# Seven 512-column GpSimd operations of a graph network kernel made into halves of 256 columns

## The chip, the cores and the metric

The kernel runs on one core of one Trainium2 chip. The metric is the device time of one launch in microseconds. The core has five engines that run side by side and meet only through semaphores: TensorE (matrix products into PSUM), VectorE, ScalarE (called ACT in the profile), GpSimd (POOL) and SyncE (SP), whose queue issues the DMAs here.

## What is computed

128 graphs, each with 128 nodes and 256 features, go through four graph layers. Each layer is preceded by a layer normalisation with relu and followed by a residual add. Cut to what matters here:

```python
h = relu(layernorm(x))                         # x: [128, 128, 256], adj: [128, 128, 128]
x = x + L0(h, adj)    # hypergraph conv 256->512, relu, layer norm over 512, conv 512->256, + its input
h = relu(layernorm(x))
x = x + L1(h, adj)    # attention: softmax of masked leaky-relu logits, times Wh, elu
h = relu(layernorm(x))
# L2: diffusion with K = 3
e = leaky_relu(sj[:, None, :] + si[:, :, None] + ab)
alpha = A * exp(e)                             # the edge mask
transition = alpha / (sum(alpha, -1) + 1e-12)
H = sum_k Xk @ Wk[k] + bk[k],  Xk = transition @ Xk
x = x + relu(H)
h = relu(layernorm(x))
x = x + L3(h, adj)    # softmax weight for each node, times a value product
```

All is float32. A large product is made of three: an operand is split into a rounded high part and the low part that is left (value minus high part), and high x high, low x high and high x low are added up in PSUM.

## The kernel before, in words

Four graphs make a group (G = 4), so a tile of a group is 128 partitions by 4 x 128 columns for an adjacency and 4 x 256 for features. There are 32 groups. The work on a group is spread over four rounds like a pipeline: in round i the engines do "next" for group i+1 (layer 0's normalisation, adjacency), "front" for group i (layers 0 and 1), "mid" for group i-1 (layer 2), "late" and "tail" for groups i-2 and i-3 (layer 3 and the store). The middle rounds are a hardware loop (`Fori`), those at both ends are written out. Each engine has a `body(r)` in which the order of its steps is written by hand, and each step waits on counting semaphores (`S[...]`). An engine works strictly in that order.

GpSimd's order within a round is: the low parts of `hT` for chunks 0 to 2 (L832; chunk 3 is VectorE's, L1086), each after ScalarE's `hT_hi` of that chunk; the reciprocal root of layer 2 (`rsqrt`: a small add L782 and a power L784); the sums of the squares `sq` (L788 twice, L841 once), each L788 after a ScalarE square of two chunks; the output add into `x4` (L846, four of 256 columns); the roots of layers 0, 3 and 4 (4 is the norm inside layer L0, `hmean`), with two small steps for `nmr` between; the edge mask `alT = zb * adj_m` (L861); four adds into `xb` (L866); the bias adds on `p0` (L794), the root of layer 1, the adds into `x3n` (L879) and `res0` (L885).

VectorE has in the same round: the layer 2 normalisation (`centred(2, ...)`: moments L973 and L977, and `h` L991, four of 256 columns), its low parts, the sums `hs` of the `hT` chunks (L1091 of 1024 columns, L1093 of 512), `wcol`, the moments of the next input, `sij`, `sjc`, the layer 4 normalisation with the same lines on `x3n`, the leaky relu of `zb` (L1070), the variance of the inner norm (L1098 to L1105), `z` (L1112) which needs the root of `hmean`, the adjacency steps of the next group (L1000 to L1010, with a 4-column copy L1004 and the products `binc_T` L1010), `p1` (L1080), `x1` (L1120) and so on.

Who needs what the changed lines make: TensorE's products on `hT_lo` (`front_w2`, L315) wait for `hT_lo`, its sums over partitions (`front_sums`, L296 on `ones` and `hsq`) for `sq_done`, and its products with the mask (`mid_ap`) for `al_ready`. TensorE's transposes (L384) wait for `h`, and its `front_c2` for `z`.

Of the kernel before, what the change touches and what calls it, by code (L numbers as in the profile page):

```python
# [7 lines left out]
ALU = mybir.AluOpType  # L8
# [56 lines left out]
def wait(eng, sem, value):  # L65

    if value is not None:
        eng.wait_ge(sem, value)


def gnn_stack(nc, x, adjT, w1T, w2T, cols, rows, l1_w, l2_wv, l2_wk, wvT, wqkT, out):
    N, C, D = x.shape
# [3 lines left out]
    G = 4  # L76
# [16 lines left out]
    with ExitStack() as ctx:  # L93
        def sb(name, *shape):
            return ctx.enter_context(nc.sbuf_tensor(name, [P, *shape], F32))

        def split(name, *shape):


            return [ctx.enter_context(nc.sbuf_tensor(f"{name}_{part}", [P, *shape], F32R)) for part in ("hi", "lo")]  # L100

        def sem(name):
            return ctx.enter_context(nc.semaphore(name))
# [23 lines left out]
        adj_m = sb("adj_m", G, C)  # L127
# [17 lines left out]
        hT = sb("hT", HC, G * C)  # L145
        hTs = split("hT", HC, G * C)
        hsq = sb("hsq", HC + 2, G * C)
        sq, hs = hsq[:, 0:HC, :], hsq[:, HC:HC + 2, :]
# [19 lines left out]
        zb = sb("zb", G, C)  # L168
        alT = sb("alT", G, C)
# [51 lines left out]
        S = {n: sem(n) for n in names}  # L221
# [555 lines left out]
        @block.gpsimd  # L777
        def _(pool):
            def rsqrt(layer, src, ready, value, mid, done):

                pool.wait_ge(ready, value)
                pool.tensor_scalar(var_e[:, layer, :], src, EPS_LN, None, ALU.add).then_inc(mid, G)  # L782
                pool.wait_ge(mid, value)
                pool.tensor_tensor(rs[:, layer, :], var_e[:, layer, :], neg_half[:], ALU.pow).then_inc(done, G)  # L784

            def add_squares(r, k):
                pool.wait_ge(S["sq_step"], r.front(2 * k + 2))
                pool.tensor_tensor(sq[:, 2 * k, :], sq[:, 2 * k, :], sq[:, 2 * k + 1, :],  # L788
                                   ALU.add).then_inc(S["sq_half"], G // 2)

            def add_bias(r, b):
                for g in (2 * b, 2 * b + 1):
                    pool.wait_ge(S["p0_copied"], r.mid(g + 1))
                    pool.tensor_tensor(p0[:, g, :], p0[:, g, :], bk[:], ALU.add).then_inc(S["p0b_ready"], 1)  # L794

            def constants():
                pool.memset(ones[:], 1.0).then_inc(S["consts_made"], 1)
                pool.memset(ident[:], 0.0).then_inc(S["pool_zero"], 1)
                pool.wait_ge(S["pool_zero"], 1)
                pool.affine_select(ident[:], ident[:], [[-1, P]], ALU.not_equal, 1.0, base=0,  # L800
                                   channel_multiplier=1).then_inc(S["consts_made"], 1)
                pool.memset(mean_w[:], 1.0 / DH).then_inc(S["consts_made"], 1)
                pool.memset(neg_half[:], -0.5).then_inc(S["consts_made"], 1)
                pool.memset(p2[:, :, D:D + 1], 1.0).then_inc(S["consts_made"], 1)
                pool.wait_ge(S["consts_made"], 5)
                pool.wait_ge(S["b2_loaded"], 16)

                pool.tensor_scalar(b2m1[:], b2m1[:], -1.0, None, ALU.add).then_inc(S["rows_used"], 1)
                pool.wait_ge(S["rows_used"], 1)

            def setup():

                def low(hi, lo, raw, n):
                    pool.wait_ge(S["weights_hi"], n)
                    pool.tensor_tensor(lo, raw, hi, ALU.subtract).then_inc(S["weights_lo"], 1)

                low(w1s[0][:], w1s[1][:], raw_w1, 1)
                low(wl1s[0][:, :, 0:D], wl1s[1][:, :, 0:D], raw_l1, 2)
                for k, at in enumerate((K2, K1, K0)):
                    low(wl2s[0][:, :, at:at + D], wl2s[1][:, :, at:at + D], raw_wk[:, k], 3 + k)  # L820
                low(wl3s[0][:], wl3s[1][:], raw_l3, 7)
                pool.wait_ge(S["weights_lo"], 6)
                pool.memset(c0[:, 4:5], 0.0).then_inc(S["set_pool"], 1)
                pool.wait_ge(S["set_pool"], 1)
                pool.wait_ge(S["set_dve"], 1)

            def body(r):
                if r.has_front:

                    for hc in range(HC - 1):  # L830
                        pool.wait_ge(S["hT_hi"], r.front(hc + 1))
                        pool.tensor_tensor(hTs[1][:, hc, :], hT[:, hc, :], hTs[0][:, hc, :],  # L832
                                           ALU.subtract).then_inc(S["hT_lo"], 1 if hc else 2)
                if r.has_mid:
                    rsqrt(2, mv[:, 2, :, 1], S["ag2"], r.mid(G), S["var2"], S["rs2_ready"])
                if r.has_front:

                    add_squares(r, 0)
                    add_squares(r, 1)
                    pool.wait_ge(S["sq_half"], r.front(G))  # L840
                    pool.tensor_tensor(sq[:, 0, :], sq[:, 0, :], sq[:, 2, :], ALU.add).then_inc(S["sq_done"], G)  # L841
                if r.has_tail:

                    pool.wait_ge(S["vw_ready"], r.tail(G))
                    for g in range(G):
                        pool.tensor_tensor(x4[:, g, :], x4[:, g, :], x3[:, g, :], ALU.add).then_inc(S["x4_ready"], 1)  # L846
                if r.has_next:
                    rsqrt(0, mv[:, 0, :, 1], S["ag0"], r.next(G), S["var0"], S["rs0_ready"])
                    pool.tensor_scalar(nmr[:, 0, :], mv[:, 0, :, 0], -1.0, None, ALU.mult).then_inc(S["nm0"], G)
                    pool.wait_ge(S["rs0_ready"], r.next(G))  # L850
                    pool.wait_ge(S["nm0"], r.next(G))
                    pool.tensor_tensor(nmr[:, 1, :], nmr[:, 0, :], rs[:, 0, :],
                                       ALU.mult).then_inc(S["nmr_ready"], G)
                if r.has_late:
                    rsqrt(3, mv[:, 3, :, 1], S["ag3"], r.late(G), S["var3"], S["rs3_ready"])
                if r.has_front:
                    rsqrt(4, hmean[:, 2, :], S["hvar_ready"], r.front(G), S["vare_h"], S["rsh_ready"])
                if r.has_mid:
                    pool.wait_ge(S["adj_m_loaded"], r.loads(r.i - 1))
                    pool.wait_ge(S["eb_ready"], r.mid(G))  # L860
                    pool.tensor_tensor(alT[:], zb[:], adj_m[:], ALU.mult).then_inc(S["al_ready"], G)  # L861
                if r.has_next:

                    pool.wait_ge(S["x_loaded"], r.loads(r.i + 1))
                    for g in range(G):
                        pool.tensor_tensor(xb[:, g, :], x_in[:, g, :], b2m1[:], ALU.add).then_inc(S["xb_ready"], 1)  # L866
                if r.has_mid:
                    add_bias(r, 0)
                if r.has_front:
                    rsqrt(1, mv[:, 1, :, 1], S["ag1"], r.front(G), S["var1"], S["rs1_ready"])  # L870
                if r.has_mid:
                    add_bias(r, 1)
                if r.has_mid:

                    wait(pool, S["h3_ready"], r.late(G))
                    wait(pool, S["x3_moved"], r.late(G))
                    pool.wait_ge(S["relu_ready"], r.mid(G))
                    for g in range(G):
                        pool.tensor_tensor(x3n[:, g, :], p0[:, g, :], x2[:, g, :], ALU.add).then_inc(S["x3_ready"], 1)  # L879
                if r.has_next:  # L880

                    for g in range(G):
                        pool.wait_ge(S["h0_ready"], r.next(g + 1))
                        pool.wait_ge(S["xb_ready"], r.next(g + 1))
                        pool.tensor_tensor(res0[:, g, :], xb[:, g, :], h0[:, g, :], ALU.add).then_inc(S["res0_ready"], 1)  # L885

            constants()
            rounds(pool, body, setup)


# [445 lines left out]
```

## Time and profile before

| what | us |
|---|---|
| median of 3 runs | 1645.03 (1644.6 to 1646.78) |
| the profiled execution | 1647.62 |
| its span | 1645.7 |
| one round of the loop in it | 48.67 |
| TensorE / VectorE / GpSimd / ScalarE busy | 1504.6 / 1408.9 / 1054.1 / 982.4 |
| granted TensorE clock, mean share of full speed | 0.979 |

The profile is of one execution of its own. Starts are in us from the start of its span, durations of single instructions are its too; times of runs are taken without it. DVE is VectorE, ACT ScalarE, POOL GpSimd, PE TensorE's products and PEld its weight loads. A number such as L832 is a line of the kernel. Where an instruction waits inside an engine (for a memory port, say), the profile shows it as a longer duration and not as idle time; a wait for a semaphore shows as idle time with the instruction that ended it.

### The profile page before, as it was taken

To read this page: it belongs to the slowest core of one execution; us is meant where nothing else is said; L and a number is where in the kernel's file an instruction comes from. 1 tells how busy PE (TensorE), PEld (TensorE's weight loads), DVE (VectorE), ACT (ScalarE), POOL (GpSimd) and SP (SyncE) were. 2 spreads that over 40 slices of the span, in tenths; PEclk is the share of its full clock that TensorE was granted. 3 is DMA by queue.
4 is the path that set the end of the run, shared out by engine and by line. 5 is a ranking of instruction groups with operands and counts; after the bars stand their busy time and mean duration, and the time that the engine had idled before them with its cause. 6 is when DMAs were issued, how large, how long until landed. Compare 5 with 4: busy or idle time off the path is not lost.

```text
span 1645.7 us, 34999 instructions
## 1 busy us (share of the span) xinstructions
PE 1504.6 (91%) x9936; PEld 1327.4 (81%) x9936; DVE 1408.9 (86%) x3980; ACT 982.4 (60%) x2153; POOL 1054.1 (64%) x1266
## 2 busy tenths in 40 slices
PE   3889999999999999999999999999999999999974
PEld 3778888888888888888888888888888888888864
DVE  6688889888889988888988888998888898888853
ACT  3345675655666665567565566656566756556643
POOL 4565676666676666667666667666766766666633
PEclk9799999999999999999999999999999999999987
DMA  4000111100111110111110011111011101001000
GB/s 144 20 15 19 46 46 33 45 31 26 45 45 45 32 45 19 38 45 45 32 45 28 30 45 45 45 32 45 15 43 45 45 32 45 26 31 45 26 26 33
DMA packets 75362, 63.21 MB, mean 38 GB/s; under 512 B 2880, under 2 KB 70848, under 8 KB 75200
## 3 DMA queue, kind: packets, MB, share of 16 engines
q1 hardware_dynamic: 75328, 62.80, 11.7%
q8 instruction: 16, 0.26, 0.1%
q14 instruction: 18, 0.15, 0.0%
HBM read 37.62 MB, written 16.78 MB: 33 GB/s over the span
## 4 chain that ended last, share of the span: by engine, by line
DVE 41%; issue 20%; PE 15%; POOL 13%; ACT 9%; DVEq 1%; POOLq 0%; ACTq 0%
DVE stats L973 6%; PE ps L311 6%; POOL rs L784 6%; POOL x L846 5%; DVE h L991 5%; PE ps L315 3%; PE ps L296 3%; DVE z L1112 3%; ACT wh L624 2%; DVE x L1120 2%; ACT pT L744 2%; DVE mv L977 2%; DVE p L1080 2%; PE ps L384 2%; DVE hsq L1091 2%
## 5 line engine op out<-in xcount | busy, mean ns | idle before, releaser
L624 ACT ACTIVATE p<-ps,rs 128x256 f32<-128x256 f32 x384 | 154.4, 478 | 225.1 <-PE ps L315 196.7
L794 POOL TENSOR_TENSOR p<-p,bk 128x256 f32<-128x256 f32 x128 | 92.8, 746 | 240.2 <-ACT p L624 240.2
L832 POOL TENSOR_TENSOR hT_lo<-hT,hT_hi 128x512 fp32r<-128x512 f32 x96 | 125.6, 1313 | 132.1 <-ACT hT_hi L641 121.1
L784 POOL TENSOR_TENSOR rs<-var_e,neg_half 128x4 f32<-128x4 f32 x160 | 187.0, 1169 | 23.7
L384 PE MATMUL ps<-ident,h 128*128 128x128 f32 x768 | 137.9, 289 | 51.4 <-DVE h L991 47.7
L311 PE MATMUL ps<-wl_hi,h2T_hi 128*128 128x256 f32 (+1 forms) x768 | 174.3, 309 | 1.4 <-DVE h2T_lo L895 1.4
L384 PEld LDWEIGHTS ps<-ident,h 128*128 128x128 f32 x768 | 83.4, 142 | 98.8 <-DVE h L991 96.6
L991 DVE TENSOR_SCALAR h<-x,mv 128x256 f32<-128x256 f32 x256 | 155.6, 627 | 2.2
L315 PE MATMUL ps<-wl_hi,h2T_lo 128*128 128x256 f32 (+1 forms) x768 | 155.5, 284 | 0.0
L311 PE MATMUL ps<-wl_lo,h2T_hi 128*128 128x256 f32 (+1 forms) x768 | 155.2, 284 | 0.0
L879 POOL TENSOR_TENSOR x3n<-p,x 128x256 f32<-128x256 f32 x128 | 100.8, 818 | 71.3 <-ACT p L737 71.3
L296 PE MATMUL ps<-p,alT 128*128 128x256 f32 (+1 forms) x512 | 127.6, 391 | 20.0 <-POOL alT L861 15.3
L296 PEld LDWEIGHTS ps<-p,alT 128*128 128x128 f32 x512 | 92.2, 189 | 52.0 <-POOL alT L861 24.6
L788 POOL TENSOR_TENSOR hsq<-hsq 128x512 f32<-128x512 f32 x64 | 124.3, 1960 | 11.3 <-ACT hsq L634 11.3
L624 ACT ACTIVATE vqk<-ps,rs 128x384 f32<-128x384 f32 x128 | 73.2, 572 | 91.9 <-PE ps L315 91.8
L311 PEld LDWEIGHTS ps<-wl_hi,h2T_hi 128*128 128x128 f32 x768 | 121.0, 191 | 3.7 <-ACT h2T_hi L677 1.5
L315 PEld LDWEIGHTS ps<-wl_hi,h2T_lo 128*128 128x128 f32 x768 | 119.3, 191 | 0.0
L311 PEld LDWEIGHTS ps<-wl_lo,h2T_hi 128*128 128x128 f32 x768 | 119.3, 191 | 0.0
L973 DVE BATCH_NORM_STATS2 stats<-x 128x6 f32<-128x256 f32 x256 | 108.7, 425 | 5.5
L641 ACT ACTIVATE hT<-ps,cols_sb 128x512 f32<-128x512 f32 x128 | 87.2, 682 | 31.3 <-PE ps L315 30.3
L846 POOL TENSOR_TENSOR x<-x 128x256 f32<-128x256 f32 x128 | 91.3, 746 | 20.5 <-ACT x L624 20.5
L311 PE MATMUL ps<-w_hi,hT_hi 128*128 128x256 f32 x512 | 89.9, 298 | 8.3 <-DVE c L960 8.3
(168 smaller groups left out, 4537.7 us busy)
## 6 DMA issues: line engine op xcount, KB each, us to landing
x_in<-in_x SPq DMA_DIRECT2D x32, 512.0 KB, 4.4
out_x<-x SPq DMA_DIRECT2D x32, 512.0 KB, 2.8
adj_f<-in_adjT SPq DMA_DIRECT2D x32, 256.0 KB, 3.5
adj_m<-in_adjT SPq DMA_DIRECT2D x32, 256.0 KB, 2.8
adj_l<-adj_m SPq DMA_DIRECT2D x32, 256.0 KB, 2.3
hsq<-in_rows SPq DMA_DIRECT2D x1, 1152.5 KB, 9.7
vqk<-in_l_wk SPq DMA_DIRECT2D x3, 256.0 KB, 8.4
x<-in_w1T SPq DMA_DIRECT2D x1, 512.0 KB, 6.3
```

The costliest lines, as they stand in the source:

```text
L296: last = pe.matmul(dst, lhsT(c), rhs(c), start=(c == 0), stop=(c == chunks - 1))
L311: pe.matmul(dst, lhsT(a, c), rhs(b, c), start=(a == b == c == 0), stop=False)
L315: last = pe.matmul(dst, lhsT(1 - late, c), rhs(late, c), start=False, stop=(c == chunks - 1))
L384: last = pe.transpose(ps[:, banks[g // 2], ((g % 2) * KC + c) * P:((g % 2) * KC + c + 1) * P], h[:, g, c * P:(c + 1) * P], ident[:])
L624: return act.activation(dst, src, ACT.Copy, scale=scale)
L784: pool.tensor_tensor(rs[:, layer, :], var_e[:, layer, :], neg_half[:], ALU.pow).then_inc(done, G)
L788: pool.tensor_tensor(sq[:, 2 * k, :], sq[:, 2 * k, :], sq[:, 2 * k + 1, :], ALU.add).then_inc(S["sq_half"], G // 2)
L832: pool.tensor_tensor(hTs[1][:, hc, :], hT[:, hc, :], hTs[0][:, hc, :], ALU.subtract).then_inc(S["hT_lo"], 1 if hc else 2)
L846: pool.tensor_tensor(x4[:, g, :], x4[:, g, :], x3[:, g, :], ALU.add).then_inc(S["x4_ready"], 1)
L879: pool.tensor_tensor(x3n[:, g, :], p0[:, g, :], x2[:, g, :], ALU.add).then_inc(S["x3_ready"], 1)
L973: dve.bn_stats(stats[:, layer, g, :], src[:, g, :]).then_inc(st, 1)
L991: dve.tensor_scalar(dst[:, g, :], src[:, g, :], mv[:, layer, g, 0:1], 0.0, ALU.subtract, ALU.max).then_inc(done, 1)
```

## The change

Every place where GpSimd worked on 512 columns in one operation within the rounds now does it in two operations of 256 columns: the three low parts of `hT`, the two sums of pairs of squares, the sum of those two, and the edge mask. These are 7 operations a round, and 14 after it. Only the last of the two signals, with the same amount as before. No wait is added or taken away, and nothing else is moved.

```diff
             def add_squares(r, k):
                 pool.wait_ge(S["sq_step"], r.front(2 * k + 2))
-                pool.tensor_tensor(sq[:, 2 * k, :], sq[:, 2 * k, :], sq[:, 2 * k + 1, :],
-                                   ALU.add).then_inc(S["sq_half"], G // 2)
+                for half in (slice(0, 2 * C), slice(2 * C, G * C)):
+                    last = pool.tensor_tensor(sq[:, 2 * k, half], sq[:, 2 * k, half], sq[:, 2 * k + 1, half], ALU.add)
+                last.then_inc(S["sq_half"], G // 2)
...
                     for hc in range(HC - 1):
                         pool.wait_ge(S["hT_hi"], r.front(hc + 1))
-                        pool.tensor_tensor(hTs[1][:, hc, :], hT[:, hc, :], hTs[0][:, hc, :],
-                                           ALU.subtract).then_inc(S["hT_lo"], 1 if hc else 2)
+                        for half in (slice(0, 2 * C), slice(2 * C, G * C)):
+                            last = pool.tensor_tensor(hTs[1][:, hc, half], hT[:, hc, half], hTs[0][:, hc, half],
+                                                      ALU.subtract)
+                        last.then_inc(S["hT_lo"], 1 if hc else 2)
...
                     pool.wait_ge(S["sq_half"], r.front(G))
-                    pool.tensor_tensor(sq[:, 0, :], sq[:, 0, :], sq[:, 2, :], ALU.add).then_inc(S["sq_done"], G)
+                    for half in (slice(0, 2 * C), slice(2 * C, G * C)):
+                        last = pool.tensor_tensor(sq[:, 0, half], sq[:, 0, half], sq[:, 2, half], ALU.add)
+                    last.then_inc(S["sq_done"], G)
...
                     pool.wait_ge(S["eb_ready"], r.mid(G))
-                    pool.tensor_tensor(alT[:], zb[:], adj_m[:], ALU.mult).then_inc(S["al_ready"], G)
+                    for g in range(0, G, 2):
+                        last = pool.tensor_tensor(alT[:, g:g + 2, :], zb[:, g:g + 2, :], adj_m[:, g:g + 2, :], ALU.mult)
+                    last.then_inc(S["al_ready"], G)
```

## Rows read from the trace of the kernel before

**Rows 1.** The page: span, busy time (share of the span) xinstructions, chain that ended last.
```profile
span 1645.7 us, 34999 instructions
...
PE 1504.6 (91%) x9936; PEld 1327.4 (81%) x9936; DVE 1408.9 (86%) x3980; ACT 982.4 (60%) x2153; POOL 1054.1 (64%) x1266
...
DVE 41%; issue 20%; PE 15%; POOL 13%; ACT 9%; DVEq 1%; POOLq 0%; ACTq 0%
DVE stats L973 6%; PE ps L311 6%; POOL rs L784 6%; POOL x L846 5%; DVE h L991 5%; PE ps L315 3%; PE ps L296 3%; DVE z L1112 3%; ACT wh L624 2%; DVE x L1120 2%; ACT pT L744 2%; DVE mv L977 2%; DVE p L1080 2%; PE ps L384 2%; DVE hsq L1091 2%
```

**Rows 2.** Busy us of two rounds; GpSimd's `xb` (busy, mean ns); `h` (ns min/median/max).
```profile
845.70:894.37 48.67, 46.16 (x312) 40.73 (x311) 43.52 (x123) 30.44 (x68) 32.65 (x39) 1.00 0.12 38
894.37:943.04 48.67, 46.18 (x312) 40.76 (x311) 43.53 (x123) 30.45 (x68) 32.63 (x39) 1.00 0.11 38
...
L866 POOL TENSOR_TENSOR xb<-x_in,b2m 128x256 f32<-128x256 f32 x128 | 89.5, 732 | 0.0
...
L991 DVE TENSOR_SCALAR h<-x,mv x256: 320/354/1372, 64.1 to 1587.0; 128x256 f32<-128x256 f32 x128
```

**Rows 3.** Waits: who waited for whom: us in total, times, longest us.
```profile
PEld ps L384 <- DVE h L991: 96.6, 163, 4.6
...
DVE z L1112 <- POOL rs L784: 41.5, 30, 1.6
...
PEld ps L296 <- POOL alT L861: 24.6, 29, 1.0
```

**Rows 4.** Timeline of one round, GpSimd: start us, us, what, [idle before].
```profile
857.76 1.29 POOL L832 TENSOR_TENSOR hT_lo<-hT,hT_hi 128x512 fp32r<-128x512 f32 x1
...
859.04 1.28 POOL L832 TENSOR_TENSOR hT_lo<-hT,hT_hi 128x512 fp32r<-128x512 f32 x1
...
876.71 1.29 POOL L861 TENSOR_TENSOR alT<-zb,adj_m 128x512 f32<-128x512 f32 x1
877.95 2.80 POOL L866 TENSOR_TENSOR xb<-x_in,b2m 128x256 f32<-128x256 f32 x4
```

**Rows 5.** Timeline of the same round, VectorE, the four `h` of layer 2.
```profile
858.02 1.18 DVE L991 TENSOR_SCALAR h<-x,mv 128x256 f32<-128x256 f32 x1
...
859.54 0.93 DVE L991 TENSOR_SCALAR h<-x,mv 128x256 f32<-128x256 f32 x1
...
860.86 0.35 DVE L991 TENSOR_SCALAR h<-x,mv 128x256 f32<-128x256 f32 x1
```

**Rows 6.** Timeline of the same round: first square sum on GpSimd, first `z` on VectorE.
```profile
863.49 2.25 POOL L788 TENSOR_TENSOR hsq<-hsq 128x512 f32<-128x512 f32 x1 [0.33 <-ACT hsq L634]
...
876.86 0.88 DVE L1112 SCALAR_TENSOR_TENSOR z<-ps,rs,bw 128x256 f32<-128x256 f32 x2 [1.39 <-POOL rs L784]
```

**Rows 7.** Timeline of the same round, VectorE, the sums of `hT`.
```profile
863.39 1.20 DVE L1091 TENSOR_TENSOR hsq<-hT 128x1024 f32<-128x1024 f32 x1
...
864.69 1.60 DVE L1093 TENSOR_TENSOR hsq<-hsq 128x512 f32<-128x512 f32 x1
```

**Rows 8.** Timeline, later in that round: two 256-column adds on GpSimd, two `h`.
```profile
887.61 0.73 POOL L794 TENSOR_TENSOR p<-p,bk 128x256 f32<-128x256 f32 x1 [6.85 <-ACT p L624]
...
888.30 0.77 POOL L794 TENSOR_TENSOR p<-p,bk 128x256 f32<-128x256 f32 x1
...
887.67 1.55 DVE L991 TENSOR_SCALAR h<-x,mv 128x256 f32<-128x256 f32 x2
```

**Rows 9.** Timeline of the same round: VectorE's copy and first `binc_T`, TensorE's second pair on `z`.
```profile
879.34 0.74 DVE L1004 COPY binc_T<-adj_f 128x4 f32<-128x4 f32 x1
...
882.27 0.48 PE L296 MATMUL ps<-z,gt 128*128 128x256 f32 x1 [0.31 <-DVE z L1112]
```

**Rows 10.** Timeline of the same round: root of layer 2, root of layer 0, `zb`.
```profile
861.45 1.71 POOL L784 TENSOR_TENSOR rs<-var_e,neg_half 128x4 f32<-128x4 f32 x1
...
872.08 1.04 POOL L784 TENSOR_TENSOR rs<-var_e,neg_half 128x4 f32<-128x4 f32 x1
...
872.50 0.68 DVE L1070 SCALAR_TENSOR_TENSOR zb<-zb 128x512 f32<-128x512 f32 x1
```

## The prediction

> **What bounds the kernel now.** I read the page first, then the waits, then one round of the loop instruction by instruction. The loop over graph groups repeats every 48.67 us, with the same busy times on every engine in neighbouring rounds [rows 2], so one round stands for all of them. The page has TensorE busy for 91% of the span and VectorE for 86% [rows 1], but a share is not a bound. The chain that ended last spends 41% of the span on VectorE, 20% on issue, 15% on TensorE and 13% on GpSimd, and the largest GpSimd entries in it are `rs` (L784, 6%) and `x` (L846, 5%) [rows 1]. The waits say where: VectorE's `z` waits for GpSimd's `rs` 30 times, 41.5 us in all, once a round, so 1.4 us a round; TensorE's transposes wait for VectorE's `h` (96.6 us, by the weight loads); TensorE waits for `alT`, 24.6 us [rows 3].
>
> In time order a round has three parts that matter here. First, 856.4 to 861.2: GpSimd makes the three low parts of `hT` while VectorE makes the four `h` of layer 2. Second, 863.5 to 876.7: GpSimd adds the squares and then works with hardly a gap through the output adds and four reciprocal roots; `z` starts at 876.86, when the last root is done [rows 4, 6]. In this part GpSimd is the bound, VectorE has 1.4 us to spare. Third, 876.7 to 881.4: GpSimd multiplies the mask, then adds `xb`, while VectorE prepares the next adjacency and ends in the second pair of `z`.
>
> **What a busy port costs, from the rows.** The first `h` starts at 858.02 and takes 1.18 us, while the shortest `h` of the run takes 0.32 us. It ends at 859.20, and the GpSimd operation under which it began ran from 857.76 to 859.05. The second `h` starts at 859.54, ends at 860.47, and the GpSimd operation beside it ended at 860.32 [rows 4, 5]. Both end 0.15 us after the GpSimd operation. The other way round, the first square sum starts at 863.49 under VectorE's 1024-column sum (863.39 to 864.59) and takes 2.25 us in place of the 1.29 of `alT` [rows 4]; VectorE's next sum (864.69) then waits for that one and takes 1.60 us; it ends at 866.29, 0.55 after it [rows 6, 7]. So each of the two engines waits for the end of the other's operation, and comes in between two GpSimd operations that stand back to back: this holds also where they have 256 columns (two `p` adds at 887.61 and 888.30, each holding an `h` that ends about 0.15 after it) [rows 8].
>
> **The change, part by part.** Seven operations of 512 columns a round become fourteen of 256.
>
> Price of one split. Durations: 1.29 us for the 512 columns of `alT` [rows 4], 0.73 for the 256 of `xb` [rows 2], so 0.73 x 2 - 1.29 = 0.17. By start to start: `alT` at 876.71, next operation at 877.95, 1.24; four `xb` from 877.95 to 880.75, 2.80 less the overlap of about 0.05, so 0.69 each [rows 4]; 2 x 0.69 - 1.24 = 0.13. I take 0.13, since in a series what counts is when the next can start. The Trainium skill ("Perfetto Trace Analysis", GPSIMD Engine Instruction) says to time GpSimd by the spacing of starts and not by reported durations. By durations the three splits below would cost 0.51 rather than 0.39, which would put the time 3 to 4 us higher.
>
> 1. Low parts (3 splits, L832). Halves start at about 856.36, 857.05, 857.76, 858.45, 859.14 and 859.83, and the last ends near 860.6 instead of 860.32; TensorE needs them for products that read `hT_lo` at about 862.0, so this costs nothing as long as that cover of over 1 us is there. What it gives: the first `h` is held by the half that ends at 858.5 and ends at 858.65 (0.55 earlier), the second asks at 859.0 and ends near 859.4 (1.1 earlier), the third asks at 859.3, under the fifth half, and ends at 860.07, the fourth asks at 860.2, under the sixth, and ends at 860.8 (0.4 earlier than 861.21) [rows 5]. The gain shrinks because GpSimd itself lasts longer. Behind the fourth `h` stand the transposes, the copies, the squares and VectorE's 1024-column sum, so the second part starts 0.40 us earlier.
>
> 2. Square sums (2 + 1 splits, L788, L841), on the path. GpSimd's work from 863.49 on is a series: wait for VectorE's sum, four halves with VectorE's second sum let in after the first, two halves more. The order doesn't change the total, only the splits do: 3 x 0.13 = +0.39. VectorE's second sum ends 0.55 earlier than it would, since it waits for a half and not for a whole; together with item 1 VectorE runs 1.0 us ahead here. That lead isn't worth anything by itself: it ends in the wait of `z` for `rs`.
>
> 3. What the lead moves. The four `h` of layer 4 now fall into four gaps between the output adds (L846) rather than one. An add that starts as an `h` ends took 0.77 in place of 0.73 [rows 8]; three more such pushes are about +0.1 on the path.
>
> 4. Edge mask (1 split, L861). `alT` ends 0.13 later. TensorE waits for it, but then reaches `z` of the second pair early, by 0.31 us (the products on `z` stand idle until 882.27) [rows 9]; this hides it. `xb` starts 0.13 later against VectorE's small copy (879.34, 0.74 us [rows 9]), which is held by an `xb` add. The copy would then be let in after the add before. The end of the last `xb` limits that gain: between -0.15 and +0.1, I take -0.05.
>
> Sum for a round: -0.40 + 0.39 + 0.10 - 0.05 = +0.04 us; over the 30 rounds that show the wait of `z`, +1.2 us. The profiled execution took 1647.6 us around a span of 1645.7 [rows 1], the median of the runs is 1645.0, 2.6 below it. So 1647.6 + 1.2 - 2.6 = 1646.2; I forecast 1646.
>
> A difference of 0.2% (3.3 us, 0.11 us a round) is about what a measurement of this kernel can tell from no change.
>
> **The rivals.**
>
> A. Slower by a new clash. With VectorE 0.7 to 1.0 us ahead, its 512-column `zb` (872.50, two inputs) would start at 871.8 to 872.2, on GpSimd's first root (872.08) or the small operation before it [rows 10]. For a root that starts while VectorE has the port the same group has a row: at 861.45, while VectorE worked on `wex` and its own `hT_lo`, it took 1.71 us in place of 1.04, +0.67. In the second part that is on the path. Against it: `zb` needs ACT's four `zb` parts, which wait for a product that stands behind the sums on TensorE, and those start only when the square sums are done. It decides if `zb` starts before about 872.2. Price 0.15 to 0.67, likeliest 0.3 a round: 1646.2 + 9 = 1655.
>
> B. Faster: the fourth `h` of layer 2 comes in before the sixth half. The halves and the `h` ask within 0.3 us of each other. Unheld it would end at 860.54, 0.67 earlier than now instead of 0.40. Then the second part starts 0.27 earlier still, -8 us: 1638. It decides if the last half starts after 860.2. If the copy of item 4 also goes ahead with its full 0.15, 1634.
>
> C. Slower: the change doesn't let VectorE in. If GpSimd's second half takes the port straight after the first, `h` waits as long as now and a little longer (+0.13 each), the gain of 0.40 is gone and the 0.39 stay: +0.5 to +0.6 a round, 1661 to 1664. Rows 8 speak against it: VectorE came in between two such adds. The Trainium skill ("SBUF — State Buffer", Who interferes with whom) has the pair taken for the whole instruction by whichever comes first and says nothing of an alternation; the trace agrees with the holding, and rows 8 go further.
>
> The outer bounds: all seven splits in series at the dearer price with nothing gained, 7 x 0.17 x 30 = 36 us, 1681; and VectorE's whole lead of 1.0 us kept round after round, 1616. Neither is in the range: the first would need GpSimd on the path also in the first part, where it has nothing due for over 1 us, the second would need `z` not to wait for `rs` [rows 3].
>
> **How the numbers follow.** Forecast (the sum near zero, -0.1 to +0.15 a round) 0.38, 1642 to 1650. A 0.25, B 0.27, C 0.10. The range takes in A and B but for their ends, and leaves out C: 1635 to 1659. Faster by over 0.2%: B, and a little of the forecast's lower end, 0.30. Slower: A but for its smallest prices, C, and a little of the upper end, 0.36. Within: 0.34. The likeliest case's own range is 1642 to 1650.
>
> **What would show it.** In the profile after: `h` of layer 2 held by at most 0.7 us, with a mean of all `h<-x,mv` well under 627 ns; L1093 near 1.0 us instead of 1.60; L788 at about 1.7 and 1.2 us for the two halves that clash and 0.73 for the others; the starts of halves 0.69 apart. `z` should still wait for `rs`, longer than before (about 2 us a round), since VectorE leads and GpSimd doesn't. If the first root after the output adds takes more than 1.04 us, it is A. If the wait of `z` for `rs` is gone, GpSimd wasn't the bound and the sum is wrong from the second part on. If `h` still takes 1.18 us, it is C.

## The result and the profile after

The changed kernel takes 1661.74 us (median of 4 runs, 1659.82 to 1662.34) against 1645.9 us (4 runs, 1644.6 to 1647.45) for the kernel before, run beside it: a ratio of 1.0094, with a 95% interval of 1.0076 to 1.0111. It is slower by 0.9%, some 16 us, where I had forecast 1646 and no change, with a range of 1635 to 1659.

The page after, with its span, busy times, and the chain that ended last. The line numbers are those of the changed kernel: what was L991 before is L998 here, and in each experiment they are that kernel's own.

```profile
span 1657.9 us, 35095 instructions
...
PE 1511.1 (91%) x9936; PEld 1332.1 (80%) x9936; DVE 1391.1 (84%) x3980; ACT 980.9 (59%) x2153; POOL 1098.7 (66%) x1490
...
POOL 40%; DVE 25%; issue 20%; PE 8%; ACT 5%; POOLq 1%; DVEq 0%; ACTq 0%
POOL rs L784 9%; POOL hsq L789 7%; POOL hT_lo L834 7%; POOL x L851 5%; POOL res L892 5%; POOL x3n L886 3%; DVE stats L980 3%; PE ps L296 3%; DVE z L1119 3%; DVE h L998 3%; DVE x L1127 2%; DVE p L1087 2%; PE ps L311 2%; DVE p L1137 2%; PE ps L384 2%
```

The busy times move in opposite ways: VectorE loses 18 us, GpSimd gains 45. Part of both is holding: an operation is held when its duration in the profile is longer than that of the same operation elsewhere, because it waits inside its engine for an operation of the other engine. The chain, 13% GpSimd before [rows 1], is 40% GpSimd now. A round of the loop, from one `gt` of VectorE to the next, lasts 49.18 us in place of 48.67 [rows 2]:

```profile
851.63:900.81 49.18, 46.40 (x312) 40.91 (x311) 43.05 (x124) 30.43 (x68) 34.06 (x46) 1.00 0.11 37
```

The waits (us in total, times, longest) that answer to rows 3:

```profile
DVE z L1119 <- POOL rs L784: 52.1, 30, 2.0
...
PEld ps L384 <- DVE h L998: 80.6, 162, 4.8
...
PEld ps L296 <- POOL alT L867: 37.0, 27, 1.4
```

So TensorE waits 16 us less for `h` in all, and none of that reaches the end: `z` waits for GpSimd's root longer than before, 52.1 us in place of 41.5.

Now the round that begins at 851.63. That of rows 4 to 10 begins at 845.69, so I take 5.94 off to compare the two, and call the result the older time. VectorE first, start and duration: the four `h` of layer 2 (one row has two), then its second `hT` sum:

```profile
863.95 0.63 DVE L998 TENSOR_SCALAR h<-x,mv 128x256 f32<-128x256 f32 x1
...
864.92 1.14 DVE L998 TENSOR_SCALAR h<-x,mv 128x256 f32<-128x256 f32 x2
...
866.19 0.61 DVE L998 TENSOR_SCALAR h<-x,mv 128x256 f32<-128x256 f32 x1
...
870.28 1.04 DVE L1100 TENSOR_TENSOR hsq<-hsq 128x512 f32<-128x512 f32 x1
```

The first `h` takes 0.63 us in place of 1.18. The last ends at 866.80, which is 860.86 in the older time, 0.35 earlier than 861.21 [rows 5]. The second sum takes 1.04 in place of 1.60 [rows 7]. VectorE is then 0.90 ahead of the older round.

GpSimd in the same round, from the square sums to the mask:

```profile
869.01 4.30 POOL L789 TENSOR_TENSOR hsq<-hsq 128x256 f32<-128x256 f32 x4 [0.26 <-ACT hsq L634]
873.39 1.43 POOL L845 TENSOR_TENSOR hsq<-hsq 128x256 f32<-128x256 f32 x2
874.77 3.02 POOL L851 TENSOR_TENSOR x<-x 128x256 f32<-128x256 f32 x4
877.76 0.27 POOL L782 TENSOR_SCALAR var_e<-mv 128x4 f32<-128x4 f32 x1
878.17 1.29 POOL L784 TENSOR_TENSOR rs<-var_e,neg_half 128x4 f32<-128x4 f32 x1
```

The output adds start at 874.77, 868.83 in the older time: just where they started before (868.84). The first square sum itself starts 0.42 earlier, but it lies under VectorE's 1024-column sum, which ends 0.36 earlier; these 0.35 are spent on the three splits in the squares. From here on it is loss. The adds last 3.02 in place of 2.85, and the root behind them takes 1.29 us in place of 1.04 [rows 10]. VectorE's rows beside that root:

```profile
877.33 0.61 DVE L998 TENSOR_SCALAR h<-x3n,mv 128x256 f32<-128x256 f32 x1
877.86 0.68 DVE L1077 SCALAR_TENSOR_TENSOR zb<-zb 128x512 f32<-128x512 f32 x1
...
883.19 0.48 DVE L1119 SCALAR_TENSOR_TENSOR z<-ps,rs,bw 128x256 f32<-128x256 f32 x1 [1.79 <-POOL rs L784]
...
885.58 0.26 DVE L1010 TENSOR_SCALAR cnt<-cnt 128x4 f32<-128x4 f32 x1
885.76 0.77 DVE L1011 COPY binc_T<-adj_f 128x4 f32<-128x4 f32 x1
```

`zb` runs from 877.86 to 878.54, and the root starts at 878.17, in the midst of it; before, `zb` started 0.42 after the root had [rows 10]. `z` starts at 883.19, 877.25 in the older time, 0.39 later than 876.86 [rows 6]. After that another 0.11 is lost at the small `cnt` step and the copy. The sum is 0.50, of the 0.51 by which the round is longer.

### The profile page after: what moved, and what is told of

Its sections match the earlier page's. It is cut to its first block, busy times and chain, and to the rows that moved or that the text cites. A ratio compares the mean times of both kernels' runs of the same rounds, so it can differ in the third digit from the quotient of the medians.

```text
span 1657.9 us, 35095 instructions
## 1 busy us (share of the span) xinstructions
PE 1511.1 (91%) x9936; PEld 1332.1 (80%) x9936; DVE 1391.1 (84%) x3980; ACT 980.9 (59%) x2153; POOL 1098.7 (66%) x1490
## 4 chain that ended last, share of the span: by engine, by line
POOL 40%; DVE 25%; issue 20%; PE 8%; ACT 5%; POOLq 1%; DVEq 0%; ACTq 0%
POOL rs L784 9%; POOL hsq L789 7%; POOL hT_lo L834 7%; POOL x L851 5%; POOL res L892 5%; POOL x3n L886 3%; DVE stats L980 3%; PE ps L296 3%; DVE z L1119 3%; DVE h L998 3%; DVE x L1127 2%; DVE p L1087 2%; PE ps L311 2%; DVE p L1137 2%; PE ps L384 2%
## 5 line engine op out<-in xcount | busy, mean ns | idle before, releaser
L834 POOL TENSOR_TENSOR hT_lo<-hT,hT_hi 128x256 fp32r<-128x256 f32 x192 | 142.1, 767 | 126.8 <-ACT hT_hi L641 118.3
L784 POOL TENSOR_TENSOR rs<-var_e,neg_half 128x4 f32<-128x4 f32 x160 | 193.8, 1211 | 24.1 <-POOL var_e L782 0.5
L384 PE MATMUL ps<-ident,h 128*128 128x128 f32 x768 | 142.4, 289 | 41.7 <-DVE h L998 39.2
L998 DVE TENSOR_SCALAR h<-x,mv 128x256 f32<-128x256 f32 x256 | 143.9, 582 | 2.3
L789 POOL TENSOR_TENSOR hsq<-hsq 128x256 f32<-128x256 f32 x128 | 135.5, 1087 | 9.1 <-ACT hsq L634 9.1
L851 POOL TENSOR_TENSOR x<-x 128x256 f32<-128x256 f32 x128 | 95.8, 778 | 20.3 <-ACT x L624 20.3
L1119 DVE SCALAR_TENSOR_TENSOR z<-ps,rs,bw 128x256 f32<-128x256 f32 x128 | 55.6, 475 | 52.2 <-POOL rs L784 52.1
```

Source lines behind the costliest of these rows:

```text
L384: last = pe.transpose(ps[:, banks[g // 2], ((g % 2) * KC + c) * P:((g % 2) * KC + c + 1) * P], h[:, g, c * P:(c + 1) * P], ident[:])
L789: last = pool.tensor_tensor(sq[:, 2 * k, half], sq[:, 2 * k, half], sq[:, 2 * k + 1, half], ALU.add)
L834: last = pool.tensor_tensor(hTs[1][:, hc, half], hT[:, hc, half], hTs[0][:, hc, half], ALU.subtract)
L998: dve.tensor_scalar(dst[:, g, :], src[:, g, :], mv[:, layer, g, 0:1], 0.0, ALU.subtract, ALU.max).then_inc(done, 1)
```

## The experiments

**Theory 1** is the account of the prediction: GpSimd's series from the first square sum to the root that `z` waits for is the bound in that stretch, and GpSimd and VectorE hold each other up for whole operations, so what a split does depends on where it stands. **Theory 2**, the rival: each added operation costs the same wherever it stands, and the changed kernel is slow because there are seven more. The first four kernels tell them apart, the next three test what the bound is worth, and the last one takes the splitting further. In the diffs a part that isn't mentioned is as in the kernel before or, where it says so, as in the whole change.

**Only the low parts halved.**

```diff
 for hc in range(HC - 1):
     pool.wait_ge(S["hT_hi"], r.front(hc + 1))
-    pool.tensor_tensor(hTs[1][:, hc, :], hT[:, hc, :], hTs[0][:, hc, :], ALU.subtract)...
+    for half in (slice(0, 2 * C), slice(2 * C, G * C)):
+        last = pool.tensor_tensor(hTs[1][:, hc, half], hT[:, hc, half], hTs[0][:, hc, half], ALU.subtract)
+    last.then_inc(S["hT_lo"], 1 if hc else 2)
```

> Only the three low parts of hT are halved (3 more operations a round). Theory 1 (GpSimd's chain from the first square sum to z is the bound, and VectorE and GpSimd wait for each other's operation): VectorE's four h end 0.35 us earlier, as they did in the whole change, and with nothing dearer behind them everything to the end of the round moves by 0.35: round 48.33 us, about 1635 us, faster by 0.6%. Theory 2 (each added GpSimd operation costs the same wherever it stands, 0.5 us by 7, 0.07 us a round each): round 48.9, about 1652 us.

Measured: 1636.16 us against 1646.63, ratio 0.9931 (0.9914 to 0.9947). Its round lasts 48.27:

```profile
839.83:888.10 48.27, 46.14 (x312) 40.80 (x311) 43.14 (x123) 30.34 (x68) 33.08 (x42) 1.00 0.11 38
```

This is 0.40 less than before, and within 0.06 us of what theory 1 gave. Theory 2 is out: three more operations made the kernel faster. `zb` starts 0.42 after the root as it did before, since VectorE and GpSimd moved together:

```profile
865.86 1.04 POOL L784 TENSOR_TENSOR rs<-var_e,neg_half 128x4 f32<-128x4 f32 x1
...
866.28 0.69 DVE L1072 SCALAR_TENSOR_TENSOR zb<-zb 128x512 f32<-128x512 f32 x1
```

**Only the squares halved** (the two L788 and the one L841 of the whole change).

```diff
-pool.tensor_tensor(sq[:, 2 * k, :], sq[:, 2 * k, :], sq[:, 2 * k + 1, :], ALU.add)...
+for half in (slice(0, 2 * C), slice(2 * C, G * C)):
+    last = pool.tensor_tensor(sq[:, 2 * k, half], sq[:, 2 * k, half], sq[:, 2 * k + 1, half], ALU.add)
+last.then_inc(S["sq_half"], G // 2)
...
-pool.tensor_tensor(sq[:, 0, :], sq[:, 0, :], sq[:, 2, :], ALU.add)...
+for half in (slice(0, 2 * C), slice(2 * C, G * C)):
+    last = pool.tensor_tensor(sq[:, 0, half], sq[:, 0, half], sq[:, 2, half], ALU.add)
+last.then_inc(S["sq_done"], G)
```

> Only the three operations on the squares are halved. Theory 1: nothing comes earlier for GpSimd, three splits of 0.12 us stand in its chain, +0.35; VectorE leads by 0.55 behind its second hT sum, so its h fall into more of the output adds (+0.1) and zb may start on the root of layer 0 (+0.25 if so): round +0.45 to +0.7, 1659 to 1667 us. Theory 2: three splits of 0.07, round +0.2, about 1652 us.

Measured: 1668.2 us against 1646.63, ratio 1.0129 (1.0112 to 1.0146), the slowest of all, a little above the expected band of 1659 to 1667. GpSimd and `zb` in one round:

```profile
856.59:906.01 49.42, 46.49 (x312) 40.88 (x311) 43.29 (x124) 30.55 (x68) 33.51 (x42) 1.00 0.11 37
...
880.10 3.01 POOL L849 TENSOR_TENSOR x<-x 128x256 f32<-128x256 f32 x4
...
883.49 1.29 POOL L784 TENSOR_TENSOR rs<-var_e,neg_half 128x4 f32<-128x4 f32 x1
...
883.18 0.68 DVE L1073 SCALAR_TENSOR_TENSOR zb<-zb 128x512 f32<-128x512 f32 x1
```

The adds start at 880.10, that is 23.51 after the round's begin against 23.15 before: +0.36 for three splits, 0.12 each. Then come the same two extras as in the whole change: adds of 3.01 for 2.85 and a root of 1.29 for 1.04. Together 0.36 + 0.16 + 0.25 = 0.77, and the round is 0.75 longer (49.42 less 48.67). The band was exceeded because the push on the adds was larger than the 0.1 I gave it. So most of the loss of the whole change lies in the squares, and the low parts give 0.35 to 0.40 of it back.

**The whole change, mask left whole.**

```diff
-for g in range(0, G, 2):
-    last = pool.tensor_tensor(alT[:, g:g + 2, :], zb[:, g:g + 2, :], adj_m[:, g:g + 2, :], ALU.mult)
-last.then_inc(S["al_ready"], G)
+pool.tensor_tensor(alT[:], zb[:], adj_m[:], ALU.mult).then_inc(S["al_ready"], G)
```

> The whole change but for the edge mask, which stays one operation of 512 columns. Theory 1: z starts 0.39 later than before, as in the whole change, but xb follows the root as before and the small copy and cnt lose nothing more: round +0.39 in place of +0.50, about 1658 us. Theory 2: six splits of 0.07, +0.43, about 1659 us; the two don't differ in the time here, but in the rows: by theory 1 the first cnt step takes 0.17 and not 0.26 us.

Measured: 1656.96 us, ratio 1.0067 (1.005 to 1.0083), round 49.06. The steps behind `z`:

```profile
883.62 0.17 DVE L1008 TENSOR_SCALAR cnt<-cnt 128x4 f32<-128x4 f32 x1
883.70 0.73 DVE L1009 COPY binc_T<-adj_f 128x4 f32<-128x4 f32 x1
```

`cnt` takes 0.17 and the copy 0.73, as before the change, and the round is 0.12 shorter than with the split mask. That is the size of one split, and the rows show it paid by VectorE, which meets the `xb` adds later: in both kernels the copy ends with the third of them.

**The whole change, `zb` later on VectorE.**

```diff
-if r.has_mid:
-    mid_logits(r)
 if r.has_front:
     front_variance(r)
+if r.has_mid:
+    mid_logits(r)
```

> The whole change, and VectorE's leaky relu of zb put behind the four small steps of the inner variance, so that it starts about 1 us later, when the root of layer 0 has read its input. Theory 1: the root of layer 0 takes 1.04 in place of 1.29 us and z starts 0.25 earlier: round 48.93, about 1654 us. If the root still takes 1.29, it wasn't zb. Theory 2: no change against the whole change, 1662 us.

Measured: 1657.91 us, ratio 1.0066 (1.005 to 1.0083): 4 us less than the whole change, about half of what I expected. The rows say why:

```profile
878.57 1.04 POOL L784 TENSOR_TENSOR rs<-var_e,neg_half 128x4 f32<-128x4 f32 x1
879.69 0.43 POOL L854 TENSOR_SCALAR nmr<-mv 128x4 f32<-128x4 f32 x1
...
879.34 0.69 DVE L1077 SCALAR_TENSOR_TENSOR zb<-zb 128x512 f32<-128x512 f32 x1
```

The root takes 1.04 again, so it was `zb` that had made it 1.29. But `zb`, now from 879.34 to 880.03, holds the small `nmr` step instead: 0.43 for 0.24. The clash wasn't removed, it was moved one instruction on, and of the 0.25 only 0.06 is left. The rest of the 4 us comes from elsewhere: in 16 of the 31 rounds of this run the small copy behind `cnt` is let in one `xb` add earlier and takes 0.16 us in place of 0.77 (in the whole change in 4 of 31), and the second pair of `z` then follows the first after 4.41 us in place of 4.60. That is 0.11 on the mean of the rounds.

**What GpSimd's series is worth.** If it is the bound, taking operations out of it must gain. The output adds are four of 256 columns; they can be two of 512 or one of 1024. Both kernels have the halved low parts too. Rival 3 is that VectorE's layer 4 steps are as near to the bound.

```diff
-for g in range(G):
-    pool.tensor_tensor(x4[:, g, :], x4[:, g, :], x3[:, g, :], ALU.add).then_inc(S["x4_ready"], 1)
+for g in range(0, G, 2):
+    pool.tensor_tensor(x4[:, g:g + 2, :], x4[:, g:g + 2, :], x3[:, g:g + 2, :], ALU.add).then_inc(S["x4_ready"], 2)
```

> Low parts of hT halved as in the run with them alone, and the four output adds of 256 columns made into two of 512. Theory 1 (GpSimd's chain to z is the bound, a split costs 0.12 there, a merge gives it back): two operations fewer in the chain, -0.25 to -0.35 us a round against 48.28, 1626 to 1629 us, though the first h of layer 4 is held longer (about 1.3 in place of 0.9 us), since VectorE waits over 1 us for z anyway. Rival 3 (VectorE's work on layer 4 is as near to the bound, so a longer hold costs what the merge gives): no gain, 1634 to 1638.

Measured: 1639.6 us, ratio 0.996 (0.9946 to 0.9975), no gain on the low parts alone. The rows of one round:

```profile
866.69 1.20 POOL L784 TENSOR_TENSOR rs<-var_e,neg_half 128x4 f32<-128x4 f32 x1
867.98 0.57 POOL L852 TENSOR_SCALAR nmr<-mv 128x4 f32<-128x4 f32 x1
...
867.50 0.35 DVE L994 TENSOR_SCALAR h<-x3n,mv 128x256 f32<-128x256 f32 x1
867.76 0.68 DVE L1073 SCALAR_TENSOR_TENSOR zb<-zb 128x512 f32<-128x512 f32 x1
```

```diff
-for g in range(G):
-    pool.tensor_tensor(x4[:, g, :], x4[:, g, :], x3[:, g, :], ALU.add).then_inc(S["x4_ready"], 1)
+pool.tensor_tensor(x4[:], x4[:], x3[:], ALU.add).then_inc(S["x4_ready"], G)
```

> The same with one output add of 1024 columns. Theory 1: three operations fewer, -0.35 to -0.45 us a round against 48.28, 1622 to 1626 us, unless the root behind it starts while VectorE has the port (then 0.1 to 0.3 less). Rival 3: slower than with two adds of 512, since the first h of layer 4 is then held to the end of the one add.

Measured: 1637.99 us, ratio 0.9956 (0.9942 to 0.997). Neither gained, which is what rival 3 said. Only its order of the two didn't come: from one `alT` to the next, on the mean of the middle rounds, it is 48.31 us with the low parts alone, 48.45 with two adds and 48.31 with one. GpSimd and `zb` in the kernel with one add:

```profile
862.27 2.38 POOL L847 TENSOR_TENSOR x<-x 128x1024 f32<-128x1024 f32 x1
...
865.04 1.04 POOL L784 TENSOR_TENSOR rs<-var_e,neg_half 128x4 f32<-128x4 f32 x1
866.16 0.75 POOL L850 TENSOR_SCALAR nmr<-mv 128x4 f32<-128x4 f32 x1
...
866.14 0.67 DVE L1071 SCALAR_TENSOR_TENSOR zb<-zb 128x512 f32<-128x512 f32 x1
```

The one add takes 2.38 for 2.85, 0.47 gained, and `nmr`, started 0.02 after `zb`, takes 0.75 for 0.24, 0.51 lost. The gain was there and the clash with `zb` took it. With two adds 0.33 was gained and about 0.5 lost: in 12 of 20 rounds that I read it is again `nmr` alone (0.75), in the other 8 `nmr` takes 0.57 and the root 1.20. That 1.20 isn't due to `zb`, which starts 1.07 after the root and so behind its usual end. What lies over the root's end there is the last `h` of layer 4, unheld (0.35), while it takes 0.38 in the rounds with a root of 1.04; that this `h` holds the root is argued from these rows, and no run tests it. The next kernel tests the reading that `zb` takes the gain against rival 3: the one add as above, and `zb` between the third and the fourth `h` of layer 4.

```diff
 def tail(g):
+    if last and g == G - 1:
+        last()
...
-centred(3, x3n, h, r.late, S["st3"], S["ag3"], S["h3_ready"])
-if r.has_mid:
+centred(3, x3n, h, r.late, S["st3"], S["ag3"], S["h3_ready"],
+        last=(lambda: mid_logits(r)) if r.has_mid else None)
+elif r.has_mid:
     mid_logits(r)
```

> As the run with halved low parts and one output add of 1024 columns, and VectorE's zb put before the last h of layer 4, so that it would run at about 26.1 to 26.8 us of the round, after the root of layer 0 (25.55) has read its input and mostly before the small nmr step behind it (26.67). Theory 1 (the gain of the merged add went into the nmr step, which took 0.75 in place of 0.24 us because zb had the port): nmr takes 0.24 to 0.4, z comes 0.3 to 0.5 earlier, round 47.8 to 48.0 us, 1621 to 1627 us. Rival 3 (VectorE's chain over layer 4, held by the long add, is the bound now): no gain or a small loss, since the last h of layer 4 then comes 0.6 later: 1636 to 1645 us.

Measured: 1625.42 us against 1646.68, ratio 0.987 (0.9854 to 0.9887), the fastest kernel of this study.

```profile
860.62 1.04 POOL L784 TENSOR_TENSOR rs<-var_e,neg_half 128x4 f32<-128x4 f32 x1
861.74 0.32 POOL L850 TENSOR_SCALAR nmr<-mv 128x4 f32<-128x4 f32 x1
...
861.32 0.66 DVE L1073 SCALAR_TENSOR_TENSOR zb<-zb 128x512 f32<-128x512 f32 x1
861.89 0.34 DVE L994 TENSOR_SCALAR h<-x3n,mv 128x256 f32<-128x256 f32 x1
...
865.46 0.88 DVE L1115 SCALAR_TENSOR_TENSOR z<-ps,rs,bw 128x256 f32<-128x256 f32 x2 [0.94 <-POOL rs L784]
```

`zb` now starts 0.70 after the root, the root is untouched, and `nmr` takes 0.32. From one `alT` to the next it is 47.90 in place of 48.31: 0.41 less, where `nmr` gave back 0.43. Rival 3 is out: the last `h` of layer 4 moved behind `zb`, and VectorE still waits 0.94 for the root. GpSimd's series is no longer far ahead of the next bound, though: `z` now waits for the root 20 times (19.6 us) and for a product of TensorE 11 times (10.6 us).

**Smaller pieces still**, low parts in quarters of 128 columns. The diff is against the kernel with only the low parts halved.

```diff
-for half in (slice(0, 2 * C), slice(2 * C, G * C)):
+for half in (slice(g * C, (g + 1) * C) for g in range(G)):
```

> The low parts of hT in quarters of 128 columns, everything else as before. Theory 1: an h of layer 2 is held by at most about 0.4 us, GpSimd finishes the low parts about 0.4 us later than with halves, TensorE doesn't wait for them; the last h ends 0 to 0.3 us earlier than with halves: round 48.0 to 48.3 us, 1627 to 1636 us. If the price of an operation counts wherever it stands (theory 2), 9 operations more than before cost 0.6 us a round: 1665 us.

Measured: 1644.83 us, ratio 0.999 (0.9981 to 1.0). The upper end that I gave for theory 1 was missed by 9 us. GpSimd's low parts with halves (first row) and with quarters, and what follows in the kernel with quarters:

```profile
850.44 4.42 POOL L833 TENSOR_TENSOR hT_lo<-hT,hT_hi 128x256 fp32r<-128x256 f32 x6 [3.58 <-ACT hT_hi L641]
...
855.46 5.91 POOL L833 TENSOR_TENSOR hT_lo<-hT,hT_hi 128x128 fp32r<-128x128 f32 x12 [3.59 <-ACT hT_hi L641]
861.33 0.23 POOL L782 TENSOR_SCALAR var_e<-mv 128x4 f32<-128x4 f32 x1
861.71 2.15 POOL L784 TENSOR_TENSOR rs<-var_e,neg_half 128x4 f32<-128x4 f32 x1
863.83 1.29 POOL L788 TENSOR_TENSOR hsq<-hsq 128x512 f32<-128x512 f32 x1
...
859.22 0.35 DVE L993 TENSOR_SCALAR h<-x,mv 128x256 f32<-128x256 f32 x1
...
861.42 0.74 PE L315 MATMUL ps<-w_hi,hT_lo 128*128 128x256 f32 x4 [0.40 <-POOL hT_lo L833]
```

The holding of `h` did become short: the last `h` takes 0.35, unheld, and ends 4.11 us after the first low part starts, against 4.56 with halves. But GpSimd's low parts now last 5.91 us, 1.49 longer than with halves, where I had expected 0.4. They last into VectorE's own `hT_lo`, the root of layer 2 starts late and takes 2.15 us, and the squares, which in the other kernels wait for ScalarE, come straight after that root. The expectation that TensorE wouldn't wait failed too: it waits for the low parts in every round, 24.3 us in all for the weight loads, against 4.4 us in a single wait with halves. From the first low part to the end of the root of layer 0 GpSimd works with hardly a gap, and it reaches the output adds 0.11 later than with halves; the adds (2.96) and the root (1.14) take another 0.21. Together this is 0.32, and the two rounds differ by 0.29, so the rows put the loss on GpSimd's series. What TensorE's wait would have cost alone, no run separates.

## Why the prediction was wrong

The single steps, in us a round, against the loop rounds of the two traces:

| step | forecast | measured |
|---|---|---|
| 1. low parts: second part starts earlier | -0.40 | -0.35 |
| 2. three splits in the squares | +0.39 | +0.35 |
| 3. pushes on the output adds | +0.10 | +0.16 |
| rival A: `zb` on the root of layer 0 | 0 (0.3 if it comes) | +0.25 |
| rounding among the small steps to `z` | 0 | -0.02 |
| 4. mask, `xb`, copy, to the second pair of `z` | -0.05 | +0.11 |
| sum | +0.04 | +0.50 |

**The bound, the port and the price of a split were right.** Each engine came in between two halves, as rows 8 had it, so rival C didn't happen; that its 1661 is the time measured is chance. A split costs 0.12 by the spacing of starts in the runs (three for 0.36), near the 0.13 that I took, not the 0.17 of durations. VectorE's lead (1.0 forecast, 0.90 measured) was worth nothing, as said. Three readings of mine were off without consequence: 2 x 0.69 - 1.24 is 0.14 and not 0.13, B with the copy's full 0.15 gives 1635 and not 1634, and TensorE's first product on `hT_lo` starts at 862.48 and not at about 862.0.

**The step that failed is the meeting of `zb` with the root of layer 0, which the sum put at nothing and left to rival A.** It measured +0.25 us a round, the largest miss of all the terms. Two things were left undecided there: when `zb` starts in the new round, and whether ScalarE's `zb` parts hold it back. I named A with its place, its point (a start before the root has read), its sign (a first root over 1.04) and a price of 0.3, and it came with 0.25, but I gave it 0.25 of the chances. ScalarE's parts, my reason against it, held nothing: the four end at 877.67 in the trace after, 0.19 before `zb` starts, and `zb` follows straight on the last `h`. VectorE's lead of 0.7 to 1.0 us was my own number, and a start of `zb` at 871.8 to 872.2 against a root at 872.08 followed from it; the measured one is 871.92 with the root at 872.23, in the older round's time. The lead moves VectorE against a GpSimd that doesn't move, so every meeting of the two behind that point had to be replayed with the new distance. I looked at three of them (the output adds, `zb`, the copy), and kept the one that hurt most out of the sum.

**Item 3 was mis-sized**: four `h` in four gaps, with 0.16 for 0.10.

**Item 4 failed in its sign.** I expected the copy to slip in one add earlier. In most rounds it is still held to the end of the third add (0.77), and `cnt` ahead of it is held as well (0.26 for 0.17). The slip happened in only 4 of 31 rounds, and in 16 of 31 where `zb` was moved. The mask left whole undoes 0.12 of the loss. TensorE waits longer for `alT` in total (37.0 for 24.6), and yet the round grows only by what VectorE loses; this fits the 0.31 of idle time that was to hide it, but no run tests that by itself. B (the fourth `h` ahead of the sixth half) didn't come; that `h` was held for 0.61.

On size: 0.50 in each of some 30 rounds is 15 us, the measured difference is 15.8. Had A been the forecast at 0.3, the time would have been put at 1655; the rest is items 3 and 4.

## What to carry to other kernels

Splitting an operation so that another engine can come in helps where the splitting engine has time, and costs its price where that engine is itself the bound; the same edit did both here, -0.40 us a round in the low parts and +0.75 in the squares. Of those 0.75 only 0.36 is the price of the splits, the rest is new clashes. An engine that gets ahead of another is not only an unused lead: it meets the other's operations at new distances, so replay every meeting behind the change, and take what falls out as the forecast. And when removing work from a bound gains nothing, look at the durations behind it before calling it another bound: 0.47 us gained and 0.51 lost stood in neighbouring rows, and moving one VectorE operation brought the gain out.

## What the runs showed of the hardware

A GpSimd operation on 4 columns is held if it starts while VectorE works on `zb`, an operation of 512 columns with two inputs in SBUF. What it loses is what was left of `zb` at its start, less 0.12 to 0.16 us: the root of layer 0 lost 0.25 with 0.37 left (the whole change), and the `nmr` step lost 0.08, 0.19, 0.33 and 0.51 with 0.24, 0.34, 0.46 and 0.65 left.

The other way round, a root that started 0.42, 0.70 or 0.77 us before `zb` took 1.04 each time, although in the first case `zb` lies within it but for its last 0.06 us, and `zb` itself ran in its usual 0.66 to 0.69. So only the beginning of the root is exposed to `zb`, and `zb` cost the root nothing when it started behind that, which is what the fastest kernel uses. Two roots don't settle it further: the 1.20 with two output adds, where `zb` came too late to be the cause, and the 1.14 with quarters, where an `h` started 0.11 before the root and `zb` 0.16 after it.
